# Attention layer and top-6 mixture of experts: the weights of two pairs issued behind further rows, gate products of batch 2 on VectorE, and the last 12 experts' rows added by the scatter into two sums

## The chip, the cores and the metric

The kernel runs on one core of one Trainium2 chip. The metric is the device time of one execution in microseconds (us). Before the change, three runs took 265.80, 265.72 and 263.58 us, median 265.72.

## What is computed

The input is `x` of 4 batches of 256 tokens with 256 features (1024 tokens), in float32. Two layers follow, each with a residual sum and a layer norm:

```python
x = _layernorm(x + attn(x, w_in, w_out))
x = _layernorm(x + ffn(x, gate_w, w1, w2, shared_gate_up, shared_down))

# attn: per token q, k, v, a, g = split(x @ w_in.T, 5)
q = q * rsqrt(mean(q * q) + eps); k = tanh(k); a = clip(sigmoid(a + 2.0), 0.6, 0.9995)
prefix = cumprod(a_c); acc = cumsum(k * v / max(prefix, 1e-6)); states = prefix * (state + acc)
y = sigmoid(g) * (q * states) + (1.0 - sigmoid(g)) * v        # then y @ w_out.T

# ffn: E=64 experts of I=176, the best K=6 for each token
probs = softmax(x @ gate_w.T); topk_w, topk_idx = top_k(probs, 6), weights scaled to sum 1
h = silu(x @ w1[e].T); y = h @ w2[e].T; routed = sum of y over the 6 experts, by topk_w
shared = (silu(g) * u) @ shared_down.T                        # g, u = split(x @ shared_gate_up.T, 2)
return routed + shared
```

## The kernel before

Five programs run side by side, one per engine, with semaphores between them: SyncE (SP) issues nearly all loads and stores in one order, GpSimd (POOL) issues the indirect DMAs, TensorE (PE) multiplies, ScalarE (ACT) applies functions and copies, VectorE (DVE) does the rest. Each works through its list in order, and a wait holds everything behind it on that engine.

**Attention and routing, batches b = 0 to 3.** TensorE projects the five kinds (`project`, L517). ScalarE writes them into SBUF (`keep_a` to `keep_g`), with gate g in `gg` and 1 - g in `og`. VectorE runs the recurrence (`prefix`, `recur`) and joins the parts (`gate_state`, which writes `yT`). TensorE multiplies `yT` by the output weights (`attend`, L554), VectorE adds the residual and takes the moments (`moments`), ScalarE takes the root and VectorE writes the normed `x1` (`norm`, L866). TensorE transposes it (`turn_x1`, L564), ScalarE copies that to `x1T`, TensorE makes the router's logits (`logits`, L577), VectorE picks the six best (`choose`) and works out a slot for each chosen pair of token and expert (`place`, ending in `slot`, L906), for which TensorE counts earlier tokens (`ranks`). Three elementwise products of each batch (k times v, 1 - g times v, g times q) are done on GpSimd for batches 0, 1 and 2 (`gates`, L313 to L317) and on VectorE for batch 3 (L829, L841, L842). The shared experts (L609, L627) are put between these steps.

**Scatter of the token rows.** For every tile of 128 tokens and every one of the 6 choices GpSimd issues an indirect DMA (L321) that writes `x1`, its weights and identifiers into the DRAM tensor `slot_rows`, which has room for 128 rows for each of the 64 experts and was zeroed at the start. The 12 DMAs of the last two tiles are waited for by SP in three steps before it loads the first rows.

**Experts, in 32 pairs j.** SP loads a pair's rows (`load_rows`, L248, into `xg`, four pairs deep) and weights (`load_weights`, L243 and L244, twelve pairs deep; the buffers of pairs 10 and 11 lie in `hsh`, which the shared experts use before). TensorE transposes the rows (L701), multiplies by w1 (L716, L723) and w2 (L730, L736); VectorE copies the transposed rows (L988) and looks up which result row belongs to which token (`look`, into `rid`); ScalarE applies silu (L465) and writes each expert's rows, weighted, into `ysb`, eight experts deep (`weigh_y`, L472). GpSimd writes these rows by an indirect DMA to the DRAM tensor `part_rows`, each to its own place by choice and token (`put_rows`, L342). I call that a put. Rows of empty slots have an index out of bounds and are left out.

**End.** SP loads `part_rows`, six parts of 1 MB, one for each choice. The first waits for the puts to expert 58, the next ones for one more put each (L296). VectorE adds the parts onto `base`, which holds x1 and the shared experts' result (L1018). The last part is added in four pieces (`last_add`, L1024), each followed by the moments of its two tiles; ScalarE takes the root and scales, and SP stores tile by tile. A flag in `meta` tells whether an expert got more than 128 tokens; each engine reads it, and with these inputs nothing is done for it.

## Time and profile before

| | |
|---|---|
| median of 3 runs | 265.72 us |
| profiled execution | 266.17 us |
| its span, first to last instruction | 264.4 us |
| TensorE busy | 206.9 us (78%) |
| VectorE busy | 126.5 us (48%) |
| ScalarE busy | 94.2 us (36%) |
| GpSimd busy | 127.6 us (48%) |
| mean granted TensorE clock | 0.905 |
| DMA traffic | 73.61 MB, mean 278 GB/s |

The span is cut into 40 equal slices of 6.6 us. Each digit is the busy share of a slice in tenths (9 is 90% or more), for DMA that of the core's 16 DMA engines; PEclk is the clock that TensorE was granted, in tenths of full speed (2.4 GHz; 5 is 1.2 GHz).

```profile
PE   3999979929939889973999999999999999900000
DVE  1337959786867755343243333333333213026794
ACT  2244375625453272000223333333333335430024
POOL 3005252796784776760133555555555567750000
PEclk9999999986986999997799999999999999975555
DMA  7999999996733233557848999999999822289804
```

The attention and the routing fill the first 16 slices, the experts the slices from 18 to 35, and the last five hold the loading and summing of the parts. A busy share is an average: it says nothing on which engine the others wait for. That is read from timelines and from the chain of work that ended last, which goes back from the last instruction, at each step to what released it.

### The profile page before, as it was taken

What the parts mean: (1) busy time and instruction counts of PE and PEld (TensorE: products, weight loads), DVE (VectorE), ACT (ScalarE), POOL (GpSimd) and SP (SyncE); (2) the same over time, 40 slices, a digit from 0 to 9 for tenths busy, and PEclk for the clock granted to TensorE, in tenths of its full rate; (3) what the DMA queues carried; (4) which work ended last, traced back from release to release, by engine and by line L of the source; (5) the groups of instructions that cost most, each with busy time, mean ns of one, the idle gap of its engine ahead of it and who ended that gap; (6) DMA issues with size and microseconds to landing.
All of it is one profiled execution on the core that took longest, in us unless ns stands there. A gap on an engine that the chain in (4) does not pass through costs nothing.

```text
span 264.4 us, 4056 instructions
## 1 busy us (share of the span) xinstructions
PE 206.9 (78%) x1332; PEld 162.5 (61%) x1332; DVE 126.5 (48%) x385; ACT 94.2 (36%) x177; POOL 127.6 (48%) x126
## 2 busy tenths in 40 slices
PE   3999979929939889973999999999999999900000
PEld 2868757827534767852688888888888877600000
DVE  1337959786867755343243333333333213026794
ACT  2244375625453272000223333333333335430024
POOL 3005252796784776760133555555555567750000
PEclk9999999986986999997799999999999999975555
DMA  7999999996733233557848999999999822289804
GB/s 258 320 427 427 428 430 371 408 403 212 316 133 104 103 135 117 186 191 224 319 138 253 359 400 403 385 391 392 379 397 396 313 78 75 75 313 382 334 15 146
DMA packets 30199, 73.61 MB, mean 278 GB/s; under 512 B 4584, under 2 KB 15450, under 8 KB 28512
## 3 DMA queue, kind: packets, MB, share of 16 engines
q1 hardware_dynamic: 24224, 57.71, 58.8%
q0 software_dynamic: 5376, 14.56, 14.8%
q10 hardware_dynamic: 576, 1.05, 1.1%
q8 instruction: 12, 0.20, 0.3%
q14 instruction: 11, 0.09, 0.1%
HBM read 46.70 MB, written 28.70 MB: 285 GB/s over the span
## 4 chain that ended last, share of the span: by engine, by line
PE 53%; DVE 15%; DMA 11%; POOL 7%; issue 7%; ACT 4%; SPq 1%; POOLq 0%; ACTq 0%; DVEq 0%
PE bank L517 10%; PE bank L716 9%; PE bank L730 9%; PE bank L736 5%; PE bank L723 5%; PE bank L701 5%; DMA shared_mem<-part_rows 3%; PE bank L609 3%; POOL slot_rows L321 3%; DMA xg<-slot_rows 3%; DMA part_rows<-shared_mem,rid 3%; POOL part_rows L342 3%; DVE x L866 2%; PE bank L577 2%; PE bank L554 1%
## 5 line engine op out<-in xcount | busy, mean ns | idle before, releaser
L342 POOL DMA_INDIRECT part_rows<-shared_mem,rid x64 | 62.3, 973 | 56.4 <-ACT shared_mem L472 42.1
L321 POOL DMA_INDIRECT slot_rows<-x,slot x48 | 50.6, 1055 | 24.1 <-issue 13.3
L988 DVE COPY shared_mem<-bank 128x512 f32<-128x512 f32 x32 | 22.0, 688 | 70.9 <-PE bank L701 70.8
L465 ACT ACTIVATE shared_mem<-bank 128x384 f32<-128x384 f32 x32 | 15.0, 490 | 82.9 <-PE bank L723 82.9
L517 PE MATMUL bank<-xT,win 128*128 128x256 f32 x160 | 40.6, 413 | 4.4 <-DMA xT<-x_t 4.4
L517 PEld LDWEIGHTS bank<-xT,win 128*128 128x128 f32 x160 | 32.7, 208 | 10.3 <-DMA win<-w_in 4.3
L472 ACT ACTIVATE shared_mem<-bank,wts 128x256 f32<-128x256 f32 x64 | 25.4, 474 | 4.9 <-PE bank L736 4.9
L716 PE MATMUL bank<-shared_mem,w1s 128*128 128x128 f32 x192 | 24.9, 282 | 1.2 <-DVE shared_mem L988 1.2
L716 PEld LDWEIGHTS bank<-shared_mem,w1s 128*128 128x128 f32 x192 | 23.5, 198 | 1.7 <-issue 1.7
L730 PE MATMUL bank<-w2s,shared_mem 128*128 128x256 f32 x96 | 24.2, 392 | 0.0
L609 PE MATMUL bank<-x1T,guw 128*128 128x256 f32 (+3 forms) x72 | 24.1, 486 | 0.0
L701 PE MATMUL bank<-cst,xg 128*128 128x128 f32 x128 | 19.5, 291 | 5.3 <-DMA xg<-slot_rows 5.1
L701 PEld LDWEIGHTS bank<-cst,xg 128*128 128x128 f32 x128 | 14.2, 145 | 11.8 <-DMA xg<-slot_rows 6.8
L730 PEld LDWEIGHTS bank<-w2s,shared_mem 128*128 128x128 f32 x96 | 17.6, 197 | 2.3 <-issue 0.4
L609 PEld LDWEIGHTS bank<-x1T,guw 128*128 128x128 f32 (+1 forms) x72 | 13.3, 191 | 6.8 <-issue 5.3
L313 POOL TENSOR_TENSOR shared_mem<-shared_mem 128x512 f32<-128x512 f32 x3 | 3.8, 1268 | 25.7 <-ACT shared_mem L390 25.7
L736 PE MATMUL bank<-w2s,shared_mem 48*128 48x256 f32 x96 | 14.4, 409 | 0.0
L723 PE MATMUL bank<-shared_mem,w1s 128*48 128x128 f32 x192 | 13.6, 278 | 0.0
L723 PEld LDWEIGHTS bank<-shared_mem,w1s 128*48 128x48 f32 x192 | 9.8, 123 | 5.0 <-issue 4.9
L627 PE MATMUL bank<-downw,hsh 128*128 128x256 f32 (+1 forms) x48 | 10.8, 382 | 0.9 <-DVE base L919 0.9
L627 PEld LDWEIGHTS bank<-downw,hsh 128*128 128x128 f32 (+1 forms) x48 | 9.0, 190 | 2.5 <-DVE hsh L914 1.3
L564 PE MATMUL bank<-cst,x 128*128 128x128 f32 x16 | 3.1, 324 | 9.0 <-DVE x L866 9.0
(131 smaller groups left out, 270.9 us busy)
## 6 DMA issues: line engine op xcount, KB each, us to landing
slot_rows<-xg SPq DMA_DIRECT2D x1, 10752.0 KB, 35.8
xg<-slot_rows SPq DMA_DIRECT2D x32, 336.0 KB, 6.7
w2s<-w SPq DMA_DIRECT2D x24, 384.0 KB, 9.1
w1s<-w SPq DMA_DIRECT2D x24, 352.0 KB, 7.3
hsh<-w SPq DMA_DIRECT2D x4, 384.0 KB, 6.8
hsh<-w SPq DMA_DIRECT2D x4, 352.0 KB, 5.7
win<-w_in SPq DMA_DIRECT2D x5, 256.0 KB, 6.7
xT<-x_t ACTq DMA_DIRECT2D x4, 256.0 KB, 5.7
```

The source lines that it names most:

```text
L321: nc.gpsimd.indirect_dma_start(rows_dram, bass.IndirectOffsetOnAxis(ap=slot[:, n:n + 1], axis=0), x1[:, t, :], None, bounds_check=E * P - ...
L342: nc.gpsimd.indirect_dma_start(part_dram, bass.IndirectOffsetOnAxis(ap=rid[:, e:e + 1], axis=0), ysb[:, e % U, :], None, bounds_check=T * ...
L472: nc.scalar.activation(ysb[:, e % U, :], bank[4 + e % 4][:, 0:D], ACT.Copy, scale=wts[:, e:e + 1]).then_inc(y_copied, 1)
L517: last = mm(out[:, c2 * S:(c2 + 1) * S], win[:, kind, c, c2 * P:(c2 + 1) * P], xT[:, b, c, :], start=(c == 0), stop=(c == DC - 1))
L609: last = mm(bank[1 + 2 * part + u % 2][0:m, 0:t1 - t0], guw[:, c, col:col + m], x1T[:, c, t0:t1], start=(c == 0), stop=(c == DC - 1))
L627: last = mm(bank[6 + t % 2][:, 0:D], hsh[0:m, n, t * P:(t + 1) * P], downw[0:m, n, :], start=(n == 0), stop=(n == 2))
L701: last = tp(bank[j % 2][:, i * D + c * P:i * D + (c + 1) * P], xg[:, (2 * j + i) % U, c * P:(c + 1) * P], ident)
L716: mm(bank[2 + j % 2][:, i * P:(i + 1) * P], w1r[j % WP][:, w:w + IA], xgT[:, j % UP, i * D + c * P:i * D + (c + 1) * P], start=(c == 0), s ...
L723: last = mm(bank[2 + j % 2][i * ODD:i * ODD + IB, 2 * P:3 * P], w1r[j % WP][:, w + IA:w + I], xgT[:, j % UP, i * D + c * P:i * D + (c + 1) ...
L730: mm(bank[4 + (2 * j + i) % 4][:, 0:D], hT[:, j % UP, i * P:(i + 1) * P], w2r[j % WP][:, i * D:(i + 1) * D], start=True, stop=False)
L736: last = mm(bank[4 + (2 * j + i) % 4][:, 0:D], hT[r, j % UP, 2 * P:3 * P], w2r[j % WP][r, 2 * D:3 * D], start=False, stop=True)
L988: v.tensor_copy(xgT[:, j % UP, :], bank[j % 2][:, 0:2 * D]).then_inc(xt_copied, 1)
```

## The change

**Weights.** The loads of pairs 10 and 11 stood on SP's queue behind the rows of pairs 0 to 3 and ahead of those of pair 4. They now follow the rows of pairs 8 and 9, in the same loop as all later weights.

**Gate products.** The three products of batch 2 are done by VectorE, inside `recur(2)` and `gate_state(2)`, as those of batch 3 are, and GpSimd no longer does them between the scatters of tile 0 and tile 1.

**Last twelve experts.** The rows of experts 52 to 63 (`LATE = 12`) are no longer written to `part_rows`. An indirect DMA that adds (`compute_op=ALU.add`) puts them onto one of two DRAM tensors of 1024 x 256 (`late_sum`), even experts on one and odd ones on the other. Before each such DMA from expert 54 on, GpSimd waits until the one two experts earlier has landed. Since no row of `part_rows` would be written for a choice that falls on a late expert, `part_rows` (6.3 MB) and both sums (2.1 MB) are zeroed from the zeroed `xg`, behind the weights of pair 9. SP waits for it before it loads the first rows, GpSimd before its first put. The six parts are loaded whole once the puts to expert 51 have landed (the sixth still waits for the first addition). When all puts have landed, GpSimd sets `routed_done`, and SP loads the two sums in four pieces each; `last_add` adds both pieces. The index of a late row is the token alone, made by an add and a multiply in `look` in place of a multiply. The branch for the flag no longer zeroes anything.

```diff
@@ sync
+            zeros = xg[:].rearrange("p u w -> p (u w)")[:, None, 0:TT * D]
+            sp.dma_start(part_dram.rearrange("(p k n) d -> p k (n d)", p=P, k=K), zeros.broadcast_to([P, K, TT * D])
+                         ).then_inc(sums_zeroed, 16)
+            for i in range(2):
+                sp.dma_start(sum_dram[i].rearrange("(p n) d -> p (n d)", p=P), zeros[:, 0]).then_inc(sums_zeroed, 16)
+            sp.wait_ge(sums_zeroed, 48)
             sp.wait_ge(scattered, 16 * (TT - TB) * K)
...
-            sp.wait_ge(sh_y_used, TT)
-            for j in range(WP - 2, WP):
-                load_weights(j)
             for j in range(UP, E // 2):
                 sp.wait_ge(xt_ready, j - UP + 1)
                 sp.wait_ge(found_ready, (2 * (j - UP) + 1) // G + 1)
                 load_rows(j)
-                if WP <= j + 2 < E // 2:
-                    sp.wait_ge(ymm_ready, j + 2 - WP + 1)
+                if WP - 2 <= j + 2 < E // 2:
+                    if j + 2 < WP:
+                        sp.wait_ge(sh_y_used, TT)
+                    else:
+                        sp.wait_ge(ymm_ready, j + 2 - WP + 1)
                     load_weights(j + 2)
...
+            for e in range(E - LATE - U, E - LATE):
+                sp.wait_ge(put[e % U], 16 * (e // U + 1))
             for k in range(K):
-
-                if k == 0:
-                    for e in range(E - K - U + 1, E - K + 1):
-                        sp.wait_ge(put[e % U], 16 * (e // U + 1))
-                else:
-                    sp.wait_ge(put[(E - K + k) % U], 16 * ((E - K + k) // U + 1))
                 if k == K - 1:
                     sp.wait_ge(parts_used, 1)
-                for h in range(2 if k == K - 1 else 1):
...
+                sp.dma_start(parts[k], rows[k]).then_inc(parts_loaded[k], 16)
+            sp.wait_ge(parts_used, 3)
+            sp.wait_ge(routed_done, 1)
+            for g in range(TT // TB):
+                for i in range(2):
+                    sp.dma_start(parts[1 + i][:, g * CW:(g + 1) * CW],
+                                 sum_dram[i].rearrange("(p t) d -> p (t d)", p=P)[:, g * CW:(g + 1) * CW]
+                                 ).then_inc(sums_loaded[g], 16)
@@ gpsimd
-                if t == 0:
-                    gates(2)
...
+                if e < E - LATE:
+                    nc.gpsimd.indirect_dma_start(part_dram, where, ysb[:, e % U, :], None,
+                                                 bounds_check=T * K - 1, oob_is_err=False).then_inc(put[e % U], 16)
+                else:
+                    if e >= E - LATE + 2:
+                        pool.wait_ge(put[(e - 2) % U], 16 * ((e - 2) // U + 1))
+                    nc.gpsimd.indirect_dma_start(sum_dram[e % 2], where, ysb[:, e % U, :], None, compute_op=ALU.add,
+                                                 bounds_check=T - 1, oob_is_err=False).then_inc(put[e % U], 16)
@@ vector
             def recur(b):
-                if b < B - 1:
+                if b < 2:
             def gate_state(b):
-                if b < B - 1:
+                if b < 2:
...
             def last_add(g):
-                dve.wait_ge(parts_loaded[K - 1 + g // 2], 16)
-                c = slice(g * TB * D, (g + 1) * TB * D)
-                link(v.tensor_tensor(flat[:, c], flat[:, c], parts[K - 1][:, c], ALU.add))
+                dve.wait_ge(sums_loaded[g], 32)
+                c = slice(g * CW, (g + 1) * CW)
+                for i in range(2):
+                    link(v.tensor_tensor(flat[:, c], flat[:, c], parts[1 + i][:, c], ALU.add))
```

The instructions as they stand on an engine follow, each with what it waits for. On SP's queue, from the first row load (`xg`) of the expert stage, before; `hsh<-w` are the weights of pairs 10 and 11:

```order
L248 DMA xg<-slot_rows 128x2x336 [waits last_scattered1,last_scattered0,scattered]
L248 DMA xg<-slot_rows 128x2x336 [waits last_scattered3,last_scattered2]
L248 DMA xg<-slot_rows 128x2x336 [waits last_scattered5,last_scattered4]
L248 DMA xg<-slot_rows 128x2x336
L243 DMA hsh<-w 128x704 [waits sh_y_used]
L244 DMA hsh<-w 128x768
L243 DMA hsh<-w 128x704
L244 DMA hsh<-w 128x768
L248 DMA xg<-slot_rows 128x2x336 [waits found_ready,xt_ready] x7
```

The same place after:

```order
L257 DMA part_rows<-xg 768x1x2048
L260 DMA late_sum<-xg 128x2048 x2
L249 DMA xg<-slot_rows 128x2x336 [waits last_scattered0,last_scattered1,scattered,sums_zeroed]
L249 DMA xg<-slot_rows 128x2x336 [waits last_scattered3,last_scattered2]
L249 DMA xg<-slot_rows 128x2x336 [waits last_scattered5,last_scattered4]
L249 DMA xg<-slot_rows 128x2x336
L249 DMA xg<-slot_rows 128x2x336 [waits found_ready,xt_ready] x5
L244 DMA hsh<-w 128x704 [waits sh_y_used]
L245 DMA hsh<-w 128x768
L249 DMA xg<-slot_rows 128x2x336 [waits found_ready,xt_ready]
L244 DMA hsh<-w 128x704 [waits sh_y_used]
L245 DMA hsh<-w 128x768
```

Three zeroing DMAs stand ahead of the rows, and the two pairs' weights are behind the rows of pair 8 and of pair 9. On VectorE, from the end of the routing of batch 1 through the gated state of batch 2, before:

```order
L906 TENSOR_SCALAR slot<-x 128x12 [waits dstep]
L844 SCALAR_TENSOR_TENSOR shared_mem<-shared_mem 128x512 [waits gated_v_ready,gated_q_ready]
L847 TENSOR_TENSOR shared_mem<-shared_mem 128x512 [waits attn_ready,dstep]
L914 TENSOR_TENSOR hsh<-sg,bank 128x512 [waits sh_silu_ready,sh_gu_ready]
L818 TENSOR_SCALAR shared_mem<-shared_mem 128x512 [waits evac]
```

And after:

```order
L910 TENSOR_SCALAR slot<-x 128x12 [waits dstep]
L845 TENSOR_TENSOR shared_mem<-shared_mem 128x512 [waits evac]
L846 TENSOR_TENSOR shared_mem<-shared_mem 128x512 [waits dstep]
L848 SCALAR_TENSOR_TENSOR shared_mem<-shared_mem 128x512 [waits dstep]
L851 TENSOR_TENSOR shared_mem<-shared_mem 128x512 [waits attn_ready,dstep]
L918 TENSOR_TENSOR hsh<-sg,bank 128x512 [waits sh_silu_ready,sh_gu_ready]
L822 TENSOR_SCALAR shared_mem<-shared_mem 128x512 [waits evac]
```

Two products are new ahead of the gated state, in place of a wait for GpSimd. A third stands, in the same way, ahead of the recurrence of batch 2. On GpSimd, all puts before, in one row:

```order
L321 DMA slot_rows<-x,slot 8192x336 [waits slot_ready]
L321 DMA slot_rows<-x,slot 8192x336 x11
L342 DMA part_rows<-shared_mem,rid 6144x256 [waits y_copied,found_ready] x64
L352 TENSOR_LOAD meta [waits put5,put4,put6,put3,put7,put2,meta_ready,put1,put0]
L352 ISA x2
```

After, from the second put on:

```order
L349 DMA part_rows<-shared_mem,rid 6144x256 [waits y_copied,found_ready] x51
L354 DMA late_sum<-shared_mem,rid 1024x256 [waits y_copied,found_ready] x2
L354 DMA late_sum<-shared_mem,rid 1024x256 [waits put4,y_copied,found_ready]
L354 DMA late_sum<-shared_mem,rid 1024x256 [waits put5,y_copied,found_ready]
L354 DMA late_sum<-shared_mem,rid 1024x256 [waits put6,y_copied,found_ready]
L354 DMA late_sum<-shared_mem,rid 1024x256 [waits put7,y_copied,found_ready]
L354 DMA late_sum<-shared_mem,rid 1024x256 [waits put0,y_copied,found_ready]
L354 DMA late_sum<-shared_mem,rid 1024x256 [waits put1,y_copied,found_ready]
L354 DMA late_sum<-shared_mem,rid 1024x256 [waits put2,y_copied,found_ready]
L354 DMA late_sum<-shared_mem,rid 1024x256 [waits put3,y_copied,found_ready]
L354 DMA late_sum<-shared_mem,rid 1024x256 [waits put4,y_copied,found_ready]
L354 DMA late_sum<-shared_mem,rid 1024x256 [waits put5,y_copied,found_ready]
```

The last twelve go to another tensor, and ten of them wait for a put (`put4` is the semaphore of expert 52 and, at the end, of expert 60).

## Rows read from the trace of the kernel before

**Rows 1.** VectorE's timeline: start us, us, line, operation, tiles, shapes, count.

```profile
52.05 4.81 DVE L866 TENSOR_SCALAR x<-res,mv,rstd 128x256 f32<-128x256 f32 x2
...
93.35 0.90 DVE L866 TENSOR_SCALAR x<-res,mv,rstd 128x256 f32<-128x256 f32 x2
```

**Rows 2.** GpSimd's timeline, [idle before and what ended it].

```profile
53.00 1.28 POOL L313 TENSOR_TENSOR shared_mem<-shared_mem 128x512 f32<-128x512 f32 x1
...
55.44 1.27 POOL L317 TENSOR_TENSOR shared_mem<-shared_mem 128x512 f32<-128x512 f32 x1
...
93.16 0.97 POOL L321 DMA_INDIRECT slot_rows<-x,slot  x1 [0.30 <-issue]
```

**Rows 3.** TensorE's timeline, matmuls alone.

```profile
49.32 3.62 PE L517 MATMUL bank<-xT,win 128*128 128x256 f32 x16
56.92 1.12 PE L564 MATMUL bank<-cst,x 128*128 128x128 f32 x4 [3.98 <-DVE x L866]
58.73 1.97 PE L577 MATMUL bank<-gatew,x1T 128*128 128x64 f32 x8 [0.69 <-ACT x1T L405]
...
64.10 3.68 PE L609 MATMUL bank<-x1T,guw 128*128 128x512 f32 x8
67.62 1.89 PE L554 MATMUL bank<-wout,shared_mem 128*128 128x256 f32 x8
...
95.65 1.10 PE L577 MATMUL bank<-gatew,x1T 128*128 128x64 f32 x8 [0.69 <-ACT x1T L405]
...
115.97 1.13 PE L716 MATMUL bank<-shared_mem,w1s 128*128 128x128 f32 x8 [1.19 <-DVE shared_mem L988]
...
131.08 0.66 PE L701 MATMUL bank<-cst,xg 128*128 128x128 f32 x4 [0.28 <-DMA xg<-slot_rows]
```

**Rows 4.** Table by stretch: busy us (count) per engine, clock, DMA share, GB/s.

```profile
58.00:60.00 2.00, 1.31 (x7) 1.28 (x7) 0.85 (x1) 0.60 (x1) 1.50 (x2) 0.50 1.04 402
```

**Rows 5.** VectorE's timeline, 65 to 77 us.

```profile
65.88 0.17 DVE L906 TENSOR_SCALAR slot<-x 128x12 uint32<-128x12 f32 x1
...
70.27 0.69 DVE L853 TENSOR_TENSOR res<-bank,xtok 128x512 f32<-128x512 f32 x1
...
76.23 0.69 DVE L829 TENSOR_TENSOR shared_mem<-shared_mem 128x512 f32<-128x512 f32 x1
```

**Rows 6.** GpSimd's timeline: last slots, put of expert 52.

```profile
102.69 0.97 POOL L321 DMA_INDIRECT slot_rows<-x,slot  x1 [0.89 <-DVE slot L906]
...
221.08 0.97 POOL L342 DMA_INDIRECT part_rows<-shared_mem,rid  x1 [0.30 <-ACT shared_mem L472]
```

**Rows 7.** DMA issues by name: KB each, us to landing.

```profile
slot_rows<-xg SPq DMA_DIRECT2D x1, 10752.0 KB, 35.8
```

**Rows 8.** Table by stretch, as rows 4.

```profile
66.00:95.00 29.00, 23.61 (x88) 14.28 (x86) 21.18 (x58) 12.89 (x18) 20.33 (x19) 0.88 0.43 161
131.00:144.00 13.00, 12.92 (x113) 10.97 (x114) 4.90 (x22) 4.26 (x10) 4.26 (x5) 1.00 0.58 170
236.00:241.00 5.00, 0.00 (x0) 0.00 (x0) 2.32 (x2) 0.00 (x0) 0.42 (x1) 0.50 1.02 405
```

**Rows 9.** Row loads' landing, of that issued in 109 to 110 us.

```profile
xg<-slot_rows SPq DMA_DIRECT2D x1, 336.0 KB, 3.2
```

**Rows 10.** Chain that ended last: start us, us, what.

```profile
123.65 7.39 DMA xg<-slot_rows
```

**Rows 11.** Puts' median landing, issued 219:222, 180:186, 232.5:233.5 us.

```profile
part_rows<-shared_mem,rid POOLq DMA_INDIRECT x3, 2.3
...
part_rows<-shared_mem,rid POOLq DMA_INDIRECT x5, 5.5
...
part_rows<-shared_mem,rid POOLq DMA_INDIRECT x2, 6.5
```

**Rows 12.** Chain that ended last, from the landing of put 62.

```profile
241.08 8.59 DMA shared_mem<-part_rows
...
252.08 0.70 DVE base L1024
```

More of the change, by code:

```diff
@@ L46 @@
 G = 4
-LAG = 4
+LATE = 12
+CW = TB * D
 C_ID, C_TRI, C_ONE = 0, 128, 256
@@ L66, in build @@
     part_dram = nc.dram_tensor("part_rows", [T * K, D], F32).ap()
+    sum_dram = [nc.dram_tensor(f"late_sum{i}", [T, D], F32).ap() for i in range(2)]
     with ExitStack() as ctx:
@@ L203, in build @@
         routed_done = sem("routed_done")
-        over_zero = sem("over_zero")
+        sums_zeroed = sem("sums_zeroed")
         over_zidx = sem("over_zidx")
@@ L210, in build @@
         over_added = sem("over_added")
-        over_step = sem("over_step")
         sp_turn = sem("sp_turn")
-        parts_loaded = [sem(f"parts_loaded{i}") for i in range(7)]
+        parts_loaded = [sem(f"parts_loaded{i}") for i in range(6)]
+        sums_loaded = [sem(f"sums_loaded{i}") for i in range(4)]
         parts_used = sem("parts_used")
@@ L341, in put_rows @@
                 pool.wait_ge(y_copied, e + 1)
-                nc.gpsimd.indirect_dma_start(part_dram, bass.IndirectOffsetOnAxis(ap=rid[:, e:e + 1], axis=0),
-                                             ysb[:, e % U, :], None, bounds_check=T * K - 1, oob_is_err=False
-                                             ).then_inc(put[e % U], 16)
+                where = bass.IndirectOffsetOnAxis(ap=rid[:, e:e + 1], axis=0)
+                if e < E - LATE:
[6 more added lines that the diff above has]
+                                                 bounds_check=T - 1, oob_is_err=False).then_inc(put[e % U], 16)
+            pool.wait_ge(sums_zeroed, 48)
             for e in range(E):
@@ L976, in look @@
                                      ALU.is_equal))
-                link(v.tensor_tensor(same[:], same[:], xg[:, u:u + G, XI:XI + 8], ALU.mult))
-                link(v.tensor_reduce(found[:], same[:], AX_X, ALU.add))
+                if g * G < E - LATE:
+                    link(v.tensor_tensor(same[:], same[:], xg[:, u:u + G, XI:XI + 8], ALU.mult))
+                    link(v.tensor_reduce(found[:], same[:], AX_X, ALU.add))
+                else:
+                    link(v.tensor_reduce(found[:], same[:], AX_X, ALU.add))
+                    link(v.scalar_tensor_tensor(found[:], xg[:, u:u + G, XI + 7], -MISS, found[:], ALU.add, ALU.mult))
                 for j in range(G):
@@ L1015, in _ @@
             flat = base[:].rearrange("p t d -> p (t d)")
-            for k in range(K - 1):
+            for k in range(K):
                 dve.wait_ge(parts_loaded[k], 16)
```

23 lines of the change are left out of this document (3 added, 20 removed).

## The prediction, made before the changed kernel ran

> **What bounds the kernel now.** I read the chain that ended last in order of time first, then each engine's timeline where the chain hands over, then the table by stretch and the landing times of DMAs. The chain has five stretches. To 102 us VectorE, ScalarE and TensorE take turns on the attention and the routing of four batches. To 119 us it is GpSimd's scatter of the token rows, to 131 us the first loads of those rows. From 131 to about 222 us it is TensorE without a gap. Then GpSimd's scatter of expert results (one "put" per expert, 1.28 us apart) leads to the last loads, sums and layer norm. A change pays only where it shortens one of these.
>
> **Part 1, gate products of batch 2 from GpSimd to VectorE.** The two instructions that write the normed x1 of batch 1 took 4.81 us; the same pair for batch 3 took 0.90 [rows 1]. What differs is GpSimd's neighbouring work: its three elementwise products ran from 53.00 to 56.71 us, and VectorE's second instruction ended right behind them. Beside the batch 3 pair ran a scatter, not a product, and nothing was lost [rows 1, 2]. So the stall is 4.81 - 0.90 = 3.91 us, and x1 is ready at 52.95 instead of 56.86.
>
> TensorE waited for it 3.98 us, and then ran at half clock: granted clock 0.50 (1.2 of 2.4 GHz) in 58 to 60 us, where it was 1.00 before the idle. Eight small logits matmuls took 1.97 us against 1.10 at full clock for batch 3 [rows 3, 4]. Without the idle, logits come 3.9 + 0.9 = 4.8 us sooner, and the projection behind them runs at the 3.62 us for sixteen matmuls of just before. TensorE's gap before the transposes vanishes; the 1.1 us in which ScalarE copies x1T stays, and a gap of that size (idle 1.19 at 115.97, where the same row's eight matmuls took 1.13) left the clock alone [rows 3].
>
> VectorE pays for it: one product ahead of the recurrence, two more before the gated state, 0.69 + 0.03 us each, priced by the same product of batch 3 [rows 5]. The first is free: VectorE starts at 52.97, needs 0.72 + 0.72 + 1.26 and is done at 55.67, before the logits at 55.95. The routing of batch 1 then ends at 60.95 instead of 66.05 [rows 5] (5.1 sooner; 0.3 more since TensorE's ranks no longer come last). The two others cost 1.44 on the path: y of batch 2 is ready at 60.9 + 4 x 0.72 = 63.75 instead of 65.96 + 2 x 0.72 = 67.4. TensorE could start the output projection of batch 2 at 61.85 (58.3, where the ranks end, + 3.53, from 64.10 to the 67.62 of the next row, for the shared experts' first unit), so it now idles 1.9 us there; before it started at 67.62 without a wait [rows 3]. VectorE then has 0.7 for the shared product and 1.7 for the prefix, and reads the projection at 66.15 instead of 70.27 [rows 5]. **Gain 4.1 us.** From here to 102 us the order is as before, so the shift is handed on. GpSimd does not eat it: before the last twelve scatters it waited 0.89 us for the slots [rows 6], and it loses 3.8 us of products. It is nearly tight there, so the shift cannot grow behind it.
>
> Bounds: if the 1.9 us idle drops the clock, the shared experts' matmuls up to 72 us take twice their time, and some 2 us of gain are left. If TensorE's next idle (3.3 us before, 3.0 after, x1 of batch 2) no longer drops it, logits come 0.9 us sooner, but VectorE's recurrence limits this to 1.2 more in all. So 2.1 to 5.3, and I take 4.1.
>
> **Part 2, zeroing 8.4 MB** (6.3 into the put rows, 2.1 into the sums). It goes out behind pair 9's weights, at about 58 us, and is waited for by SP before the first row load and by GpSimd before the first put. The zeroing of the slot rows, 10,752 KB beside other loads, took 35.8 us [rows 7]; 8.4 MB at that rate is 28 us. From 66 to 95 us the DMA engines were 43% busy and moved 161 GB/s [rows 8]. Even begun at 71 us it ends by 99, and the first row load can go at 109.2 [rows 9] - 4.1 = 105. Cost nothing; without this cover it costs what is late beyond 105. Scatters beside it land later, but only the last ones are waited for.
>
> **Part 3, weights of pairs 10 and 11 behind rows.** SP issued four row loads, then 1.5 MB of weights (1.9 us of issue), then rows for pairs 4 and 5. Those landed 7.39 us after issue; TensorE waited 0.28 us for the second one [rows 3, 10]. After, they are issued about 2 us sooner and nothing heavy is ahead of them. TensorE is the limit then: its own work ahead of these transposes ends near 130 us, so it gets back the 0.28 and hardly more. **Gain 0.5 us** (0 to 1). Behind the moved loads on SP's queue stand row loads of pair 9 and on, which have over 10 us of room. The weights, issued near 128 to 131 us, are used 20 us later, and the stretch 131 to 144 us has room, with 58% of DMA time used [rows 8].
>
> So the put of expert 52, at 221.08 us [rows 6], moves to 221.08 - 4.6 = 216.4 (rounded down).
>
> **Part 4, the last twelve experts added by the scatter.** Each sum takes every second expert, and each add waits until the one before it on that sum has landed: six rounds in series. Before, only GpSimd's own 1.28 us stood between puts. Behind the waiting put on GpSimd stand all later ones and the flag that releases the last loads. ScalarE's copy of experts 60 to 63 waits for puts 52 to 55, TensorE hardly.
>
> What one round costs no row shows: there is no adding scatter. The nearest are plain puts, from issue to landing: 2.3 us with DMA queues quiet, 5.5 in the saturated stage, 6.5 with 1 MB loads beside them [rows 11]. An add also reads its destination. Its lower bound is no extra, its upper bound twice the plain price. I take 0.5 extra in the quiet case and 6.0 altogether in the loaded case (between 5.5 and 6.5, the reading mostly hidden in queueing), as the nearest row is the plain put. The six full loads of part rows are now all issued once put 51 lands (215.2 + 2.3 = 217.5): 6.3 MB at the 405 GB/s of 236 to 241 us [rows 8] is 15.5 us, to 233. So the rounds are 2.8, 6, 6, 4.4 (half loaded), 2.8, 2.8 = 24.8 us: 216.4 becomes 241.2, and the odd sum, 1.3 us behind, 242.5. VectorE's six additions of 2.3 us end near 236, hidden.
>
> The Trainium skill (DMA: Bandwidth & Descriptors, Rules for kernel authors) says an accumulating DMA reads its destination and writes it later; the same page of the Trainium skill (Latency and other measured facts) puts HBM access at 0.2 us on average and 2 us at high load. By an estimate from that page the rounds would be 2.5, 8, 8, 5, 2.5, 2.5 = 28.5, and the result 266.7 instead of 263.0. No row of this case shows that leg alone.
>
> **After the last put.** Before: put 62 landed at 241.08, the load took 8.59, and an addition 2.3. From 252.08 (first last_add) to the end at 264.4 are 12.3 us [rows 12]. After: the last landing, GpSimd's check of the overflow flag (no row shows it; 1 us, between nothing and the 2.3 of a quiet put), SP's issues and the landing of two loads of 256 KB (2.9 together, a little under the 3.2 of one load of 336 KB [rows 9]): 3.9 us. Then 12.3 plus four more additions of 0.72 = 15.2. Together 19.1 us. 242.5 + 19.1 = **261.6 us of span**. The profiled execution took 266.17 us for a span of 264.4, 1.8 more, and stands 0.45 above the median of 265.72: 261.6 + 1.8 - 0.45 = **263.0 us**.
>
> **Rivals.**
> (a) *The add costs a plain put*, and the front gains its upper bound: rounds 2.3, 5.5, 5.5, 3.9, 2.3, 2.3 = 21.8 from 215.2, so 258.8. For it: the landings of 2.3 are steady. Against: the extra read.
> (b) *The read leg waits under load*: quiet rounds 2.5 (hardly over a put), loaded ones 8 (loads lengthen a put by 6.5 - 2.3 = 4.2, and the add's read leg by half of that once more, 2 on 6), half loaded 5. The sum is 28.5 instead of 24.8, and the time 266.7, within 1%. For it: the same put goes from 2.3 to 6.5 when loads stand beside it [rows 11], and the change puts 6.3 MB exactly there. Against it: reads may overlap with queueing. The rule of the Trainium skill above gives the same rounds.
> (c) *Slower: every add costs twice a put.* Quiet 4.6, loaded 13: 216.4, 221.0, 234.0, then four quiet rounds to 252.4, plus 1.3 and 19.1 is 272.8 of span, 274.1 us. It decides once the six rounds exceed 27.5 us, 4.6 each: then nothing is left of the gain. From 30.2 us it is over 1% slower. For it: two transfers instead of one. Against: 128 KB is far from filling the engines in the quiet case.
> (d) *The change does not free VectorE*: scatters take the place of GpSimd's products beside the x1 pair and block it as well, or the new 1.9 us idle drops the clock. 2.1 instead of 4.1 us of front gain gives 265.0. Against it: the pair at 93.35 beside a scatter took 0.90 [rows 1, 2].
>
> **How the numbers follow.** Forecast 0.45, (a) 0.17, (b) 0.20, (c) 0.12, (d) 0.06. About 1% is what a measurement of this kernel can tell from no change: 263.1 and 268.4. The forecast straddles the first bound, 0.27 of it below and 0.18 above; with (a) 0.44, and 0.01 from (d) at its edge, faster is 0.45. From (b) 0.05 goes over the upper bound (with loaded rounds dearer still), with (c) slower is 0.17, and the rest, 0.38, is the same. The forecast's own range is 261 to 266. Range 259.5 to 270.5: it leaves out the fastest part of (a) and nearly all of (c).
>
> **What would show it.** x1 of batch 1 in 0.9 us near 52.1; clock 1.00 from 58 to 62; first put-stage TensorE work 4 to 5 us sooner; no wait on the zeroing; the moved weights without a TensorE wait near 150; adds landing 2.8 us after issue when quiet and 6 when loaded; last landing near 242.5; 19 us behind it. Wrong it is made above all by the landing time of an adding scatter, then by the clock in the stretch from 62 to 72 us.

## The result, and the profile after

The changed kernel takes **280.01 us** (median; 279.7 to 282.5 in 4 runs) against 265.76 for the kernel before beside it: 1.058 times as long, interval 1.049 to 1.066. The forecast was 263.0, and its range ended at 270.5. The profiled execution took 279.94 us with a span of 278.0 (before 266.17 and 264.4). The medians below are of all runs of a kernel, while the ratios and their intervals leave out the runs in which the chip was in a slower state, so the two can differ by up to 1%.

The front half did what was forecast. VectorE's timeline of the kernel after has the pair of instructions that write x1 of batch 1 at 0.73 us instead of 4.81 [rows 1]:

```profile
52.81 0.73 DVE L870 TENSOR_SCALAR x<-res,mv,rstd 128x256 f32<-128x256 f32 x2
53.58 0.69 DVE L833 TENSOR_TENSOR shared_mem<-shared_mem 128x512 f32<-128x512 f32 x1
```

TensorE's timeline after has no wait for x ahead of the transposes, 1.10 us for the logits instead of 1.97 [rows 3], and the idle of 1.90 us at the output projection of batch 2 that the prediction announced:

```profile
53.60 0.66 PE L568 MATMUL bank<-cst,x 128*128 128x128 f32 x4
55.52 1.10 PE L581 MATMUL bank<-gatew,x1T 128*128 128x64 f32 x8 [1.26 <-ACT x1T L409]
...
64.57 3.17 PE L558 MATMUL bank<-wout,shared_mem 128*128 128x256 f32 x8 [1.90 <-DVE shared_mem L851]
67.54 4.15 PE L613 MATMUL bank<-x1T,guw 128*128 128x512 f32 x8
```

The loss is all at the end. GpSimd's timeline after, from the put of expert 51 on, with expert 52 in the second row (before, its put stood at 221.08 [rows 6]); the bracket is the idle time ahead and what ended it:

```profile
214.13 0.97 POOL L349 DMA_INDIRECT part_rows<-shared_mem,rid  x1 [0.30 <-issue]
215.40 1.58 POOL L354 DMA_INDIRECT late_sum<-shared_mem,rid  x1 [0.30 <-ACT shared_mem L476]
217.29 1.58 POOL L354 DMA_INDIRECT late_sum<-shared_mem,rid  x1 [0.30 <-issue]
224.62 1.55 POOL L354 DMA_INDIRECT late_sum<-shared_mem,rid  x1 [5.75 <-DMA late_sum<-shared_mem,rid]
...
237.82 3.35 POOL L354 DMA_INDIRECT late_sum<-shared_mem,rid  x1 [2.21 <-ACT shared_mem L476]
```

The chain that ended last, after, from expert 53's add to the first addition of a late sum (start us, us, what):

```profile
217.29 10.30 DMA late_sum<-shared_mem,rid
...
228.43 8.56 DMA late_sum<-shared_mem,rid
...
237.82 5.48 DMA late_sum<-shared_mem,rid
...
244.61 3.71 DMA late_sum<-shared_mem,rid
...
249.15 3.71 DMA late_sum<-shared_mem,rid
...
253.70 3.73 DMA late_sum<-shared_mem,rid
...
258.68 0.32 SPq L302
259.04 3.72 DMA win<-late_sum
...
262.86 0.70 DVE base L1028
```

That is one of the two series: six adds, each issued behind the landing of the one before. Three landed after 10.30, 8.56 and 5.48 us, three after 3.7. From landing to next issue lie 0.83 to 0.86 us (217.29 + 10.30 = 227.59, issue at 228.43), once 1.31. The rounds are 11.14, 9.39, 6.79, 4.54, 4.55 and 3.73 = **40.1 us**, where the prediction had 24.8. The first is the longest. The part loads went out just ahead of this add, from 216.51 us on.

A trap in reading: GpSimd's timeline lays several of these waits on a ScalarE copy (L476), which ended 0.3 us before the issue. ScalarE itself waited there, because its copy of expert 61 needs the buffer that expert 53's add still held. In each such row the landing stands 0.8 us before the issue and ScalarE's copy lies between. The thing that was late is the landing.

### The profile page after: what moved, and what is told of

Its sections match the earlier page's. It is cut to its first block, busy times and chain, and to the rows that moved or that the text cites. A ratio compares the mean times of both kernels' runs of the same rounds, so it can differ in the third digit from the quotient of the medians.

```text
span 278.0 us, 4072 instructions
## 1 busy us (share of the span) xinstructions
PE 204.2 (73%) x1332; PEld 160.5 (58%) x1332; DVE 129.1 (46%) x393; ACT 94.3 (34%) x177; POOL 131.9 (47%) x123
## 4 chain that ended last, share of the span: by engine, by line
PE 49%; DMA 17%; DVE 15%; issue 6%; ACT 5%; POOL 5%; POOLq 0%; ACTq 0%; SPq 0%; DVEq 0%
DMA late_sum<-shared_mem,rid 13%; PE bank L720 9%; PE bank L734 9%; PE bank L521 9%; PE bank L705 6%; PE bank L740 5%; PE bank L727 5%; POOL slot_rows L328 3%; PE bank L558 2%; DVE base L1028 2%; PE bank L581 2%; DMA win<-late_sum 1%; DMA xT<-x_t 1%; DVE bst L1030 1%; DMA xg<-slot_rows 1%
## 5 line engine op out<-in xcount | busy, mean ns | idle before, releaser
L349 POOL DMA_INDIRECT part_rows<-shared_mem,rid x52 | 50.4, 969 | 50.7 <-ACT shared_mem L476 39.1
L521 PE MATMUL bank<-xT,win 128*128 128x256 f32 x160 | 39.6, 406 | 4.4 <-DMA xT<-x_t 4.4
L521 PEld LDWEIGHTS bank<-xT,win 128*128 128x128 f32 x160 | 32.0, 204 | 10.2 <-DMA win<-w_in 4.4
L476 ACT ACTIVATE shared_mem<-bank,wts 128x256 f32<-128x256 f32 x64 | 25.6, 474 | 15.0 <-DMA late_sum<-shared_mem,rid 11.0
L354 POOL DMA_INDIRECT late_sum<-shared_mem,rid x12 | 20.4, 1704 | 19.7 <-ACT shared_mem L476 8.9
L320 POOL TENSOR_TENSOR shared_mem<-shared_mem 128x512 f32<-128x512 f32 x2 | 2.5, 1260 | 26.4 <-ACT shared_mem L394 26.4
L1028 DVE TENSOR_TENSOR base<-base,xT 128x512 f32<-128x512 f32 x4 | 2.7, 680 | 23.1 <-DMA win<-late_sum 23.1
L499 ACT ACTIVATE fstd<-fmv,cst 128x2 f32<-128x2 f32 x4 | 1.2, 295 | 31.3 <-DVE fmv L1032 31.3
```

The costliest lines, as they stand in the source:

```text
L349: nc.gpsimd.indirect_dma_start(part_dram, where, ysb[:, e % U, :], None, bounds_check=T * K - 1, oob_is_err=False).then_inc(put[e % U], 16)
L354: nc.gpsimd.indirect_dma_start(sum_dram[e % 2], where, ysb[:, e % U, :], None, compute_op=ALU.add, bounds_check=T - 1, oob_is_err=False).t ...
L476: nc.scalar.activation(ysb[:, e % U, :], bank[4 + e % 4][:, 0:D], ACT.Copy, scale=wts[:, e:e + 1]).then_inc(y_copied, 1)
L521: last = mm(out[:, c2 * S:(c2 + 1) * S], win[:, kind, c, c2 * P:(c2 + 1) * P], xT[:, b, c, :], start=(c == 0), stop=(c == DC - 1))
```

## Experiments

**Each part alone.** Four kernels, all beside the kernel before at 265.96 us. The edits are pieces of the diff shown above. Gates alone:

```diff
-                if t == 0:
-                    gates(2)
...
-                if b < B - 1:
+                if b < 2:
```

> The kernel before with the products of batch 2 on VectorE only. Theory 1: the pair of instructions that writes x1 of batch 1 takes 0.7 to 0.9 us instead of 4.8, the last slots are ready about 4 us sooner, and the time is about 261 to 262 us. Theory 2: the stall is owed to something else than the three products on GpSimd, and stays; then within 1 us of before.

Measured 261.38 us, 0.986 of before (0.980 to 0.993): 4.6 us by the medians, as theory 1 had it. The first of GpSimd's last twelve scatters of token rows, which waits for the last slots, was issued 5.0 us sooner than at 102.69 [rows 6]:

```profile
97.73 0.97 POOL L321 DMA_INDIRECT slot_rows<-x,slot  x1 [0.88 <-DVE slot L904]
```

Order of the weight loads alone (the second piece of the diff of SP's queue):

> The kernel before with the weights of pairs 10 and 11 behind further rows only. Theory 1 (forecast 0.5 us, and the trace of the changed kernel points to 1.5): TensorE does not wait for the rows of pairs 4 and 5, time 264 to 265.3 us. Theory 2: the rows of pairs 2 and 3 also come sooner without 1.5 MB of weights at their heels, and the gain is up to 2 us. Theory 3: weights arrive late for pair 10 and TensorE waits near 150 us: no gain or slower.

Measured 263.46 us, 0.992 (0.988 to 0.996): 2.5 us by the medians, and 1.3 in the trace, where the last put stands at 234.16 instead of 235.44. TensorE's matmuls in 100 to 145 us that waited for rows, first before, then with this edit:

```profile
122.47 1.11 PE L701 MATMUL bank<-cst,xg 128*128 128x128 f32 x4 [4.09 <-DMA xg<-slot_rows]
124.32 1.11 PE L701 MATMUL bank<-cst,xg 128*128 128x128 f32 x4 [0.73 <-DMA xg<-slot_rows]
```

```profile
122.39 2.07 PE L701 MATMUL bank<-cst,xg 128*128 128x128 f32 x8 [4.16 <-DMA xg<-slot_rows]
```

The wait of 0.73 us at 124.32 is gone, and the 0.28 at 131.08 [rows 3] as well: 1.0 us. The second is the wait for the pair 5 rows, which theory 1 named. The first, counted at four transposes a pair, is that for pair 3, whose rows had the weights right behind them: theory 2. The time lies just under the range of theory 1.

Both of them, without the late sums:

> The kernel before with two parts of the change only: products of batch 2 on VectorE, weights of pairs 10 and 11 behind further rows. Theory 1 (the front gained as in the trace of the changed kernel, and the adding scatter alone lost it again): the last put is issued about 5 to 6 us sooner than the 235.44 us of before, and the time is about 260 us, 5 to 6 under before. Theory 2 (the earlier end of the expert stage is owed to the late experts' DMAs or to the zeroing, not to these two edits): within 2 us of before.

Measured **260.52 us**, 0.978 (0.971 to 0.985). This is faster than both kernels of the case. The last put is issued at 229.57, 5.9 us sooner than before, as theory 1 had it.

The late sums alone, with their zeroing and loads:

> The changed kernel with the products of batch 2 back on GpSimd and the weights of pairs 10 and 11 back ahead of the rows of pair 4: the zeroing and the late experts' adding scatter alone. Theory 1 (series of adds costs it all): put 52 at about 221 us, the last add lands about 42 us behind it, near 263, and the time is about 285 us, 19 to 20 over before. Theory 2 (the loss comes from adds that collide with an expert stage moved 6 us forward): clearly under 280 us.

Measured 284.67 us, 1.070 (1.064 to 1.076), and theory 1 had 285. The whole loss, and more, is in the late sums: 18.7 us by the medians, of which the two other edits take back 4 to 5.

**What makes the late sums slow.** Four kernels, all beside the kernel before at 266.32 us. First the same order and the same waits, but plain writes:

```diff
-  nc.gpsimd.indirect_dma_start(sum_dram[e % 2], where, ysb[:, e % U, :], None, compute_op=ALU.add,
+  nc.gpsimd.indirect_dma_start(sum_dram[e % 2], where, ysb[:, e % U, :], None,
```

> The changed kernel with the last 12 experts' rows written by the same scatter in the same order and with the same waits, but plainly, not added (the sums then keep only the last row written to each token). Theory 1 (the add is what costs): a plain put landed 2.3 us after issue in a quiet queue and 5.5 to 6.5 us under the load of the part loads in the kernel before, and the scatter behind a landing starts 0.84 us later, so the six rounds are about 7.3, 7.3, 7.3, 3.1, 3.1 and 2.3, 30 us in sum, the last landing is at about 247 us and the time about 269 us. Theory 2 (the series is what costs, whatever the operation): the rounds stay at 11, 9, 7, 4.5, 4.5 and 3.7, the last landing at 257 and the time at 279 to 281 us. Each scatter's own time on GpSimd tells which of the two set the 1.55 us: 0.97 us by theory 1.

Measured 268.99 us (1.013 of before, 0.994 to 1.031), span 266.1. Theory 1 had 269. The chain of this kernel:

```profile
215.44 7.19 DMA late_sum<-shared_mem,rid
222.77 0.71 issue
223.48 7.02 DMA late_sum<-shared_mem,rid
...
240.20 2.31 DMA late_sum<-shared_mem,rid
...
243.37 2.35 DMA late_sum<-shared_mem,rid
```

The last landing is at 245.7, against 257.4 with adds. A put in the quiet queue takes 2.3 us and an add 3.7; beside the part loads 7.1 and 8.6 to 10.3. GpSimd's own part is 0.97 and 1.55. The six rounds of this chain take 30.3 us (215.44 to 245.7) instead of 40.1. So in them the add costs about 10 us over a plain write.

Next, the adds as they are, but the part loads wait until the last add has landed:

```diff
-            for e in range(E - LATE - U, E - LATE):
+            for e in range(E - U, E):
```

> The changed kernel with the six part loads held back until the last adds have landed, so that the adds run with nothing else in the queues but the last expert rows' traffic. Theory 1 (an add costs 3.7 us quiet, and the part loads beside it stretch it to 8 to 10 us): every add lands 3.7 to 4 us after issue, the six rounds are 4.6 x 5 + 3.7 = 27 us or are set by the experts' rows coming (2.3 us each, which is less), the last landing is at about 244 to 246 us, 12 us earlier than with the loads beside them; the part loads (6 MB in six transfers) then start there and the span ends 16 to 20 us of loads and about 15 us of tail later, 278 to 284 us in all. Theory 2 (the first rounds are long for a reason of their own, such as first use of the add): the landings stay at 10.3, 8.6 and 5.5 us with no load beside them, and the time is over 290 us.

Measured 281.21 us. Its chain (every pause of 0.70 us is the larger part of the 0.84 us between a landing and the next issue):

```profile
215.32 3.71 DMA late_sum<-shared_mem,rid
219.18 0.70 issue
219.87 3.55 DMA late_sum<-shared_mem,rid
...
240.25 3.76 DMA late_sum<-shared_mem,rid
244.09 4.81 DMA xtok<-part_rows
```

From the add of expert 52 to the last landing, at 244.0, are 28.7 us: the price of the two series with no part loads beside them. With the part loads beside them it is 42.0 us, to 257.4. So 13.3 us of the 42.0 come with those loads and with what VectorE does once they have landed (below). Holding the loads back gains nothing in the total, since they then stand on the path themselves.

What an add takes from the DMA engines shows in GpSimd's own queue. This is the queue's row for 220 to 244 us of this kernel, in which ten adds were issued (packets, MB, share of 16 engines), and then for 236 to 245.9 us of the kernel with plain writes, five puts:

```profile
q0 software_dynamic: 1529, 1.03, 38.2%
```

```profile
q0 software_dynamic: 288, 0.59, 17.0%
```

38.2% of 24 us over ten adds is 0.9 us of all sixteen engines each, 17.0% of 9.9 over five puts 0.34. An add is cut into some 150 packets, a put into some 58.

Then four sums instead of two:

```diff
-                    if e >= E - LATE + 2:
-                        pool.wait_ge(put[(e - 2) % U], 16 * ((e - 2) // U + 1))
-                    nc.gpsimd.indirect_dma_start(sum_dram[e % 2], ...
+                    if e >= E - LATE + 4:
+                        pool.wait_ge(put[(e - 4) % U], 16 * ((e - 4) // U + 1))
+                    nc.gpsimd.indirect_dma_start(sum_dram[e % 4], ...
```

> The changed kernel with four sums instead of two, so that an add waits for the fourth before it at most two of the last 12 adds' waits are in each series of three; two more 1 MB sums are zeroed, loaded and added. Theory 1 (latency in series): three rounds of 10.3, 5 to 7 and 4, behind the experts' rows, end at about 237 to 241 us; the four sums' loads (4 MB) take 4 us more than two, and 8 more additions of 512 KB pieces about 5.8 us, so the time is about 268 us (265 to 272). Theory 2 (the add's traffic itself is limited, a read and a write of every row): 12 adds take the same time however many are in flight, the last landing stays at 250 us or later, and the time is over 283 us.

Measured 280.33 us, span 279.0. Both theories missed, theory 2 by less (249.1 and 280.3 us, where it had 250 or later and over 283). The last landing came 8.3 us sooner than after the change, though only half as many adds stand in series. More of the twelve adds now fall beside the part loads, which raises the median landing from 4.0 to 10.1 us. Beside the loads each also took somewhat longer: the adds issued in 220 to 224 us landed after 11.4 us in the median and those in 224 to 232 after 12.4, where the longest in the chain of the changed kernel took 10.3. The gain was spent behind the last landing: 8.9 us instead of 5.4 to the first late addition, and eight more additions of 0.7 us.

Last, the twelve scatters written plainly to rows of their own, with no wait between them. The late rows are left out of the sum:

> The changed kernel with the last 12 experts' rows written plainly, each to its own row of a third tensor, with no wait of one scatter for another; these rows are left out of the output sum, the loads and additions of the two sums stay. Theory 1 (adds in series cost 23 us over plain independent puts): the scatters follow the experts' rows 2.3 us apart as before, the last is issued at about 230 us and lands at 237, the sums' loads start at about 238 us instead of 258.7, and the time is 258 to 261 us. Theory 2 (the late rows are late because the six part loads now start at 216 us and fill the queues): the last landing is at 245 us or later and the time 267 us or more, without any add or series.

Measured 263.77 us (0.988 of before, 0.983 to 0.992), 3 us over the version without late sums. (That one ran on another chip with 0.978 of before, 0.971 to 0.985, so the two intervals touch.) The last landing was at 242.2. Neither theory had it. No wait and no add is left, yet GpSimd's timeline shows the last scatter 22.7 us behind the first, where 11 x 1.28 = 14.1 was due:

```profile
215.66 0.97 POOL L353 DMA_INDIRECT late_rows<-shared_mem,rid  x1 [0.30 <-ACT shared_mem L475]
...
222.05 2.94 POOL L353 DMA_INDIRECT late_rows<-shared_mem,rid  x1 [0.30 <-issue]
225.29 0.97 POOL L353 DMA_INDIRECT late_rows<-shared_mem,rid  x1 [0.30 <-issue]
226.57 2.66 POOL L353 DMA_INDIRECT late_rows<-shared_mem,rid  x1 [0.30 <-issue]
...
238.32 2.47 POOL L353 DMA_INDIRECT late_rows<-shared_mem,rid  x1 [0.31 <-issue]
```

VectorE's timeline of the same kernel has the additions of the parts beside them:

```profile
221.85 2.29 DVE L1020 TENSOR_TENSOR base<-base,xtok 128x2048 f32<-128x2048 f32 x1 [2.42 <-DMA xtok<-part_rows]
226.09 2.29 DVE L1020 TENSOR_TENSOR base<-base,xT 128x2048 f32<-128x2048 f32 x1 [1.95 <-DMA xT<-part_rows]
```

Each long scatter begins inside an addition and ends 0.85 us behind it (221.85 + 2.29 = 224.14; 222.05 + 2.94 = 224.99). Six of the twelve are long, and the additions are what the change moved beside them. But the queues were full at that time too. Two more kernels separate the two, with one run each, on a chip where the kernel before took 278.99 us:

```diff
                 dve.wait_ge(parts_loaded[k], 16)
+                if k == 1:
+                    for u in range(U):
+                        dve.wait_ge(put[u], 16 * (E // U))
```

> The version with independent plain scatters, with VectorE's additions of the parts held back, from the second on, until the last scatter has landed; five of the six part loads still run beside the scatters. As in that version, the late rows are left out of the sum. Theory 1 (VectorE's additions block GpSimd while it makes descriptors): only the scatter beside the first addition, near 222 us, takes over 2 us; the other eleven take 0.97, and the last one is issued 11 x 1.28 + 2 us behind the first, at about 231 us instead of 238.3. Theory 2 (full DMA queues hold the scatter up): five of the twelve still take 2.2 to 2.9 us, and the last is issued at about 237 us. The time itself is longer either way, since five additions, 11.5 us, now come behind the last landing.

GpSimd's late scatters in this kernel, whose first addition on VectorE ran at 241.04 for 2.30 us:

```profile
241.01 0.97 POOL L353 DMA_INDIRECT late_rows<-shared_mem,rid  x1 [3.24 <-ACT shared_mem L475]
242.29 1.89 POOL L353 DMA_INDIRECT late_rows<-shared_mem,rid  x1 [0.31 <-issue]
...
251.29 0.98 POOL L353 DMA_INDIRECT late_rows<-shared_mem,rid  x1 [0.30 <-issue]
```

Only the scatter that began inside that addition is long. The one at 241.01, begun 0.03 us before it, took 0.97, and so did the ten others (0.97 or 0.98), nearly all of them while the loads ran. So VectorE's additions do it, not the queues. Theory 1 missed the last issue: it stood 20.9 us behind the first, since on this chip GpSimd waited up to 3.24 us for ScalarE's copies in between. (The time, 285.04 us, has five additions behind the last landing and says nothing here.) It is the pattern of the x1 pair [rows 1, 2] the other way round: there GpSimd's products held VectorE up.

The same hold in the changed kernel:

> The changed kernel with the same hold: the adds run in two series beside the part loads, but without VectorE's additions, from the second on. Theory 1 (VectorE's additions only lengthen an add's own time on GpSimd): the add that took 3.35 us takes 1.55, the last landing is about 2 us earlier than in the changed kernel, 40 us of rounds become 38, and the loaded landings of 10 and 8.5 us stay. Theory 2 (the additions also delay the landing itself, since the descriptors of an add come in pieces): the loaded landings fall to 6 us or less and the rounds to about 30 us.

Measured 300.12 us, for the same reason. The loaded landings stayed, at 9.05 and 8.83 us in its chain:

```profile
232.03 9.05 DMA late_sum<-shared_mem,rid
241.92 8.83 DMA late_sum<-shared_mem,rid
251.59 3.69 DMA late_sum<-shared_mem,rid
```

From the add of expert 53 (233.92) to the last landing (267.56 + 3.71 = 271.27) are 37.35 us, against 40.1. The rounds are 2.8 us shorter. The one add that the changed kernel issued inside an addition accounts for 1.8 of them (3.35 instead of 1.55 on GpSimd); whether the rest is the additions' or this chip's, one run doesn't show. The loaded landings don't come from the additions, as theory 1 had it; with the quiet version they are the part loads'.

**Fewer late experts.** LATE = 4 and LATE = 8, on a chip where the kernel before took 284.08 us:

> The changed kernel with the last 4 experts' rows added into the sums instead of 12, so each sum gets two adds in series. Theory 1 (a series of adds, each stretched by the loads): the eight puts that move back to plain ones run 1.28 us apart and the part loads start when the one of expert 59 lands, at about 227 us; the first adds are issued at about 226 and 228 us and land 10 us later under the loads, the second ones land 7 to 9 us after that, at about 246 us; with 5.4 us to the first last addition and 15.2 us behind it the span is about 267 us and the time 269 us (265 to 272). Theory 2 (only the long series costs, two rounds hide behind the part loads, which take 16 us from 227 us): the last landing is at or before 243 us, the sums' loads follow the part loads at once, and the time is 264 us or less, no slower than the kernel before.

> The changed kernel with the last 8 experts' rows added into the sums, so four adds in series per sum. Theory 1 (each round adds its own latency: about 10, 9, 5 and 3.7 us with 0.84 us between them, from about 222 us): last landing at about 252 us and a time of 273 to 276 us, between the versions with 4 and with 12. Theory 2 (a fixed price for using the sums at all, whatever the number of rounds): the same time as with 4 or with 12, within 2 us.

Measured 292.26 us (1.027 of before, 1.020 to 1.034) and 294.84 (1.039, 1.032 to 1.046). By the ratios they lie in order below the 1.058 of twelve, as theory 1 had it; its times were for a chip like the first. The landings in the chain of the version with eight are 10.14, 7.36, 4.85 and 3.72 us, those of the version with four 10.77 and 7.72. Since this chip was slower for all, the version with four was run again beside the one without late sums, where the kernel before took 279.80:

> The kernel before with the gates of batch 2 and the order of the weight loads changed, and no late rows: the version that was fastest so far, again, beside the next one on one chip. Theory 1: 0.978 of the kernel before (0.97 to 0.985), since the gain sits between 52 and 132 us and the end of the kernel is as before. Theory 2 (its first ratio was a chip's): 0.99 or more.

> The changed kernel with 4 late experts, two adds in series per sum, on the same chip as the version without late rows. Theory 1: two rounds of 10.8 and 7.7 us under the part loads, plus the sums' loads and 2.9 us of further additions: 14 to 19 us more than the version with no late rows on the same chip (the first run of this kernel had 1.027 of before where that version had 0.978, on a chip where before itself took 284 us). Theory 2 (the first run's ratio came from that chip): within 6 us of the version with no late rows.

Measured 277.82 us without late sums (0.984, 0.974 to 0.993) and 289.57 with four late experts (1.035, 1.029 to 1.041). The first gain holds up on a second chip, somewhat smaller, within the intervals. The second kernel is 11.8 us behind it by the medians and 5%, some 14 us, by the ratios: at or just below the 14 to 19 of theory 1, and far above the 6 of theory 2. Even two rounds do not hide; the chain with four late experts:

```profile
247.22 9.48 DMA late_sum<-shared_mem,rid
...
258.01 8.20 DMA late_sum<-shared_mem,rid
```

## Why the prediction was wrong

**Part 1 held.** Gain 4.1 forecast; alone it measured 4.6 us in the time and 5.0 in the trace, and in the changed kernel the last slots came 3.7 us sooner (99.01 instead of 102.69). The 1.9 us of idle came as worked out. Whether it drops TensorE's clock was left as a bound, and it did so in some kernels and not in others. The table by stretch, in 64 to 72 us, for the kernel after and for gates alone (the last three columns are granted clock, DMA share, GB/s):

```profile
64.00:72.00 8.00, 7.12 (x16) 3.99 (x16) 4.73 (x10) 2.17 (x3) 5.99 (x6) 0.79 1.02 417
```

```profile
64.00:72.00 8.00, 5.03 (x17) 2.43 (x15) 5.32 (x13) 2.19 (x4) 6.12 (x7) 1.00 0.74 284
```

The kernel after ran part of it at half clock (1.2 of 2.4 GHz; granted clock 0.50 in 66 to 68 us), gates alone at full clock, behind the same idle of 1.90 us. Of the kernels whose code is the same up to here but for zeroing, the plain-write and the four-sums versions stayed at 1.00 too, the quiet and the independent ones fell to 0.79. With the drop the last slots came at 99.0 to 99.6 us, without it at 97.7 to 98.5: about 1 us, not the 2 of the bound. Rival (d) happened in part and was small.

**Part 2 held.** Row loads went out at 105.47 us, as forecast (105), and the plain independent version, which zeroes and loads the sums like the others, lost only 3 us in all. The DMA engines, fully busy in 90 to 94 us of the kernel after (share 1.01), were at 0.30 in 98 to 102, which fits the forecast end by 99. Zeroing was hidden.

**Part 3 was mis-sized:** 0.5 us forecast (0 to 1), 1.0 to 1.3 in the trace, and by ratio 0.4 to 1.2% of the time. The step counted only the wait at 131.08 and left out the 0.73 us at 124.32, which vanished too. The put of expert 52 stood at 215.40 us; 216.4 was forecast. Of these 5.7 us, 3.7 are the slots' and 1.0 to 1.3 the weights'; the rest, under 1 us, isn't traced.

**Part 4 failed, at "What one round costs".** Quiet rounds were put at 2.8 us and loaded ones at 6.0, "as the nearest row is the plain put". Measured, the quiet round is 4.55: 3.71 of landing and 0.84 from the landing to the next issue. That gap the prediction left out altogether, though every step of a series pays it. The loaded rounds are 11.14, 9.39 and 6.79. The sum is 40.1 instead of 24.8, so 15.3 of the 16.4 us by which the span of 278.0 missed 261.6.

The overlap was wrong too. The first round was counted as quiet, 2.8 us, but the part loads left just before it, and its 11.14 us alone are 8.3 of the 15.3. Split by operation, the plain price itself was too low: the version with plain writes needs 30.3 us for the same six rounds, 5.5 more than was forecast for adds, with landings of 7.0 to 7.2 beside the loads and the same gap. The other 9.8 us are the add's: the prediction had priced an operation that reads and writes by one that only writes.

The upper bound that the part itself gave, twice the plain price, has the measured quiet round, 4.6, but by luck: it holds 4.6 of landing and no gap, where 3.7 and 0.84 were measured.

Rival (c), with rounds of 4.6 and one of 13, foresaw the place, the sign and, by 6 us, the size (274.1), with the same luck and with one loaded round where there were three; its threshold of 30.2 us was passed by 10. It was given 0.12. Rival (b) named the load as what lengthens the adds, which the quiet version shows, but took it for 2 us on 6. The Trainium skill (DMA: Bandwidth & Descriptors, Latency and other measured facts), as used for (b), pointed the right way with HBM access at up to 2 us under load; the estimate of 28.5 us of rounds that the prediction worked out from it is refuted by the 40.1.

**After the last put,** 3.9 us were forecast from the last landing to the first late addition and 5.4 measured: GpSimd's check of the flag and SP's wake-up took 1.25 instead of 1.0 (257.43 to 258.68), and the first loads, with SP's issues, 4.2 (258.68 to 262.86) instead of 2.9. The tail behind, 15.1 us, was forecast at 15.2.

**What the late sums could have given.** Even free of adds and of series the scheme brought 263.77 us, not less than the 260.52 without it. In the kernel before, the puts run before VectorE's additions (last put at 235.44, first addition at 236.45) and all but the last few before the part loads (from 231.14). The change puts both beside the last twelve puts, and pays for it with six long scatters. Then come two additions of 0.7 us where one stood, for each of four pieces. This account of the difference is read from the traces; no run takes the items apart. That the scheme might bring nothing even then was not among the rivals.

Open is why an add's landing grows from 3.7 to 10 us where a put's grows from 2.3 to 7. The engine time and packets of an add fit that it gives more work to queues that the part loads fill, but no run changed one without the other.

## What to carry over

Before putting dependent DMAs in series, price one round as landing plus wake-up plus issue of the operation itself, and price it beside whatever the same change starts at that moment. Where no row shows the operation, carry both of its bounds through the sum and let the range hold both, in place of trusting the row that looks most alike: here they gave 263 and 274 us, and the range left the second out. Work that a change makes ready earlier is not free: look which engine it then runs beside.

## What the hardware showed that was not expected

- A GpSimd scatter that adds takes 1.55 us of GpSimd instead of 0.97, lands after 3.7 us instead of 2.3 in quiet queues, and takes about 0.9 us of all 16 DMA engines instead of 0.34.
- VectorE's addition of two SBUF tiles (128 x 2048, 2.29 us) holds up a scatter that GpSimd begins in the meantime, to 0.85 us behind its own end: 1.9 to 2.9 us in the rows above instead of 0.97, and 3.35 instead of 1.55 for an add. One that had begun just before it wasn't held up. The Trainium skill (SBUF — State Buffer, Who interferes with whom) describes the pair of ports that VectorE and GpSimd share as an exclusive lock, which whoever issues first gets for the whole instruction, and the other engine as blocked; these rows agree. The same section of the Trainium skill tells of a `tensor_tensor` that did not stall a DMA; VectorE's addition is one, and here it did hold up the scatter.
- From a landing to the next GpSimd scatter that waits for it are 0.84 us, where GpSimd isn't busy with another.
- With the same instructions on TensorE up to that point and the same idle of 1.90 us, its clock fell to 0.50 in three kernels (after, quiet, independent writes) and stayed at 1.00 in four (gates alone, both edits, plain writes, four sums).
